# Transposes of shifted attention scores split by upper and lower 64 rows, each half into its own PSUM bank

## The reference

```python
x = jnp.roll(input, (-SH, -SH), axis=(1, 2))      # windows of 7 x 7 = 49 tokens, 16 per image
qkv = x @ qkv_weight.T + qkv_bias                 # 8 heads of 8 channels
attn = jnp.einsum('whnd,whmd->whnm', q * scale, k) + relative_position_bias
attn = attn + attn_mask                           # shifted-window mask
attn = jax.nn.softmax(attn, axis=-1)
out = jnp.einsum('whnm,whmd->whnd', attn, v)      # then projection, roll back
```

## Time and profile before

| | |
|---|---|
| Median of 3 runs | 204.85 us (204.46 to 205.53) |
| Profiled execution, its own time | 204.72 us |
| Span of the profiled execution | 202.9 us |
| TensorE busy | 189.9 us, 2827 matmuls |
| Turns (L892) | 256 transposes, 33.1 us busy |
| Exponentials (L583) | 64, 28.4 us busy |
| Values (L912) | 1024 passes, 29.0 us busy |
| Scores (L881) | 512 passes, 28.2 us busy |
| Granted TensorE clock | 0.999 |

### The profile page before, as it was taken

The page is one execution under the profiler, slowest core; times in us unless marked ns, Lnnn a source line. Parts: engine busy times, 40 slices in busy tenths (PEclk is TensorE's granted clock), DMA queues, the critical chain, the costliest instruction groups (busy, mean ns, idle before and its releaser), DMA issues.

```text
span 202.9 us, 7030 instructions
## 1 busy us (share of the span) xinstructions
PE 189.9 (94%) x2827; PEld 132.7 (65%) x2830; DVE 154.7 (76%) x319; ACT 142.1 (70%) x305; POOL 110.7 (55%) x123
## 2 busy tenths in 40 slices
PE   7769999999999999999999999989979899999994
PEld 2447888888888878788878787645536566443331
DVE  4476689977887877886876977897768848874894
ACT  2148698688778789878887964537746547798880
POOL 0338999958311549823279305925993631635680
PEclk9999999999999999999999999999999999999999
DMA  6980000000000010100010100022132551020124
GB/s 198 438 357 3 3 3 3 3 3 5 0 3 3 3 26 6 40 3 3 3 26 3 43 5 3 3 64 45 26 68 66 122 128 30 20 77 2 44 78 160
DMA packets 6111, 10.77 MB, mean 53 GB/s; under 512 B 960, under 2 KB 5184, under 8 KB 5952
## 3 DMA queue, kind: packets, MB, share of 16 engines
q1 hardware_dynamic: 5648, 9.72, 15.8%
q10 hardware_dynamic: 432, 0.60, 0.9%
HBM read 5.03 MB, written 1.61 MB: 33 GB/s over the span
## 4 chain that ended last, share of the span: by engine, by line
PE 60%; POOL 13%; ACT 11%; issue 6%; DMA 5%; DVE 2%; SPq 2%; POOLq 1%; ACTq 0%; DVEq 0%
PE turned L892 12%; PE scores L881 10%; PE outs L912 10%; PE scores L1021 4%; PE qkv L862 4%; PE qkv L852 4%; PE scores L1037 2%; POOL v L420 2%; DMA xw<-xw_in 2%; POOL h L413 2%; POOL v L418 2%; ACT xs L694 2%; PE outs L936 2%; ACT pt L583 2%; DMA p<-parts 2%
## 5 line engine op out<-in xcount | busy, mean ns | idle before, releaser
L1298 DVE TENSOR_REDUCE mx<-scores 113x16 f32<-113x784 f32 x32 | 30.9, 964 | 6.9 <-PE scores L881 6.6
L374 POOL TENSOR_TENSOR rstd<-ve,mhalf 128x1 f32<-128x1 f32 (+1 forms) x15 | 9.6, 641 | 46.7 <-DVE ve L1264 46.4
L892 PE MATMUL turned<-cst,d 113*113 113x113 f32 x256 | 33.1, 272 | 0.0
L225 POOL TENSOR_TENSOR kex<-ks,cst 128x784 f32<-128x784 f32 (+1 forms) x16 | 23.6, 1475 | 17.3 <-ACT ks L562 17.1
L892 PEld LDWEIGHTS turned<-cst,d 113*113 113x113 f32 x256 | 27.9, 178 | 7.1 <-issue 7.1
L583 ACT ACTIVATE pt<-turned 113x392 f32<-113x392 f32 x64 | 28.4, 496 | 5.7 <-PE turned L892 3.1
L1303 DVE TENSOR_TENSOR d<-scores,mx 113x784 f32<-113x784 f32 x32 | 31.2, 976 | 1.1
L553 ACT ACTIVATE scores<-rel 113x784 f32<-113x784 f32 x32 | 26.2, 818 | 5.7 <-POOL rel L366 3.2
L881 PE MATMUL scores<-kex,qs 32*49 32x196 f32 x512 | 28.2, 332 | 2.0 <-DVE kex L225 1.7
L912 PEld LDWEIGHTS outs<-vsb,pt 113*49 113x49 f32 x1024 | 26.0, 125 | 5.6 <-issue 2.5
L912 PE MATMUL outs<-vsb,pt 113*49 113x18 f32 x1024 | 29.0, 199 | 0.0
(11 more groups left out here) (139 smaller groups left out, 379.0 us busy)
## 6 DMA issues: line engine op xcount, KB each, us to landing
p<-parts SPq DMA_DIRECT2D x14, 112.5 KB, 2.3
x<-x_in SPq DMA_DIRECT2D x1, 1568.0 KB, 10.0
out<-xw SPq DMA_DIRECT2D x8, 196.0 KB, 1.9
xw<-xw_in SPq DMA_DIRECT2D x1, 784.0 KB, 6.7
xs<-xs SPq DMA_DIRECT2D x6, 98.5 KB, 2.1
v2x<-v SPq DMA_DIRECT2D x6, 98.0 KB, 2.1
ker<-ker_in SPq DMA_DIRECT2D x2, 288.0 KB, 10.2
p3x<-parts SPq DMA_DIRECT2D x8, 60.0 KB, 2.0
```

The lines of the kernel that those rows point to most:

```text
L225: return engine.tensor_tensor(kex[:, par, :, a * WT:b * WT], ks[:, a * WT:b * WT].rearrange("p (o t) -> p o t", o=1).broadcast_to([P, 4, n ...
L892: mm = pe.transpose(ps_t[j][0:WK, n * P:n * P + WK], d[0:WK, k % 2, h:h + 2, :].rearrange("p a b -> p (a b)")[:, 0:WK], ident[0:WK, 0:WK])
L1298: dve.tensor_reduce(top, sc, AXX, ALU.max).then_inc(max_done, 1)
```

## The change

A turn becomes one call per pair. It does 16 transposes: for each of 8 couples of blocks one over the partitions 0 to 48 (the one image) into the bank `ps_t[0]`, and one over the partitions 64 to 112 (the other image) into `ps_t[1]`, in alternation. Each result is a block of 49 columns, stored 64 apart. An exponential `expo(k, w)` now reads one bank, which holds one image's queries for all heads and both windows, and writes its 49 columns of every block of `pt`; the layout of `pt` is as before. `t_done` counts one per pair, both exponentials wait for the whole turn, and a turn waits for both exponentials of the pair before.

```diff
--- before.py
+++ after.py
@@ -575,13 +575,13 @@
                         ps_qk[q, 0:NW * C].rearrange("p (a n d) -> p a n d", a=NW, d=HD), ACT.Identity)
                 last.then_inc(v_ready, 1)
 
-            def expo(k, j):
-
-                act.wait_ge(t_done, 2 * k + j + 1)
+            def expo(k, w):
+
+                act.wait_ge(t_done, k + 1)
                 if k >= 2:
                     act.wait_ge(pv_done, k - 1)
-                act.activation(pt[0:WK, k % 2, j].rearrange("p n (w t) -> p n w t", w=2),
-                               ps_t[j][0:WK, :].rearrange("p (n w t) -> p n w t", n=4, w=2)[:, :, :, 0:WT],
+                act.activation(pt[0:WK, k % 2, :, :, w * WT:(w + 1) * WT].rearrange("p j n t -> p (j n) t"),
+                               ps_t[w][0:WK, :].rearrange("p (n t) -> p n t", n=NH)[:, :, 0:WT],
                                ACT.Exp).then_inc(exp_done, 1)
 
             def evac_att(R):
@@ -883,15 +883,16 @@
                                            start=False, stop=True, skip_group_check=True)
                 mm.then_inc(s_done, 1)
 
-            def turn(k, j):
+            def turn(k):
                 pe.wait_ge(sub_done, k + 1)
                 if k > 0:
-                    pe.wait_ge(exp_done, 2 * k - 1 + j)
-                for n in range(4):
-                    h = 8 * j + 2 * n
-                    mm = pe.transpose(ps_t[j][0:WK, n * P:n * P + WK],
-                                      d[0:WK, k % 2, h:h + 2, :].rearrange("p a b -> p (a b)")[:, 0:WK],
-                                      ident[0:WK, 0:WK])
+                    pe.wait_ge(exp_done, 2 * k)
+                for n in range(NH):
+                    for w in range(2):
+                        q = slice(64 * w, 64 * w + WT)
+                        mm = pe.transpose(ps_t[w][0:WK, 64 * n:64 * n + WT],
+                                          d[q, k % 2, 2 * n:2 * n + 2, :].rearrange("p a b -> p (a b)")[:, 0:WK],
+                                          ident[q, q])
                 mm.then_inc(t_done, 1)
 
             def values(k):
@@ -953,8 +954,7 @@
                 R, p = k // 2, k % 2
                 g, r = R // NW, R % NW
 
-                turn(k, 0)
-                turn(k, 1)
+                turn(k)
                 if p == 0 and R + 2 < NR:
                     proj_qk(R + 2)
                 if p == 0 and R >= 2:
@@ -1137,16 +1137,14 @@
             pe.wait_ge(w2_ready, 2)
             pe.wait_ge(ld_late, 16)
             pe.wait_ge(g12_ready, 1)
-            turn(NP - 2, 0)
-            turn(NP - 2, 1)
+            turn(NP - 2)
             project(NR - 3)
             values(NP - 3)
             conv1_quad(0)
             sums_quad(0)
             pe.wait_ge(gn_copied, nth(1, 2))
             gather(NR - 2)
-            turn(NP - 1, 0)
-            turn(NP - 1, 1)
+            turn(NP - 1)
             values(NP - 2)
             values(NP - 1)
             sums_quad(1)
@@ -1299,7 +1297,7 @@
                 dve.wait_ge(max_done, k + 1)
 
                 if k >= 2:
-                    dve.wait_ge(t_done, 2 * k - 2)
+                    dve.wait_ge(t_done, k - 1)
                 dve.tensor_tensor(d[0:WK, s].rearrange("p (j m) t -> p j m t", j=2)[:, :, :, 0:WT], sc,
                                   top.rearrange("p j (m o) -> p j m o", o=1).broadcast_to([WK, 2, NH, WT]),
                                   ALU.subtract).then_inc(sub_done, 1)
```

## The result

The kernel after takes 207.25 us (median of 4 runs, 207.06 to 208.21), beside 204.82 (204.46 to 205.53) for the kernel before: a ratio of 1.0126, 95% interval 1.0103 to 1.0150. 208.7 was predicted, with a range of 203.8 to 213. The profiled execution takes 207.32 with a span of 205.4, so 2.5 us more span than before. In the kernel after, the turn's line is L893; the attention's TensorE lines behind it are one higher (L926 for L925), those of the later blocks are the same, and VectorE's are two lower.

A forecast was written before the change was run, and what follows sets the result against it. TensorE, busy 94% of the span, was taken as the bound. Terms 1.9 + 1.6 + 0.45 - 0.05 - 0.1 + 0.1 = 3.9 us on 204.72 gave 208.6, as a median 208.7; range 203.8 to 213, forecast's own 207.3 to 210.3.

The forecast's parts named there:

- The cadence: Turn's transposes on TensorE: 8 steps of a side-by-side pair at 0.099 us, so a turn stays 0.79 us.
- The pause and the open load: TensorE after a turn: shape change pauses, next line's load no longer hidden; loss 0.13 to 0.14 us before L852.
- even turn: Turns followed by L852 or L936 on the chain, pairs 2 to 28: 14 x 0.135 = 1.9 us lost.
- odd turn: Turns followed by L925's transposes, pairs 3 to 29: 0.09 to 0.135 each, taken 0.115; 14 x 0.115 = 1.6 us lost.
- Mix turns: Turns behind a small full-array matmul (L816 or L983), 5 before 121 us: a new pause, 5 x 0.09 = 0.45 us.
- The waits: Both exponentials wait for all 16 transposes, the first 0.34 us later; V's wait for Q's copy just covered, by 0.05.
- the two late stretches: 68 to 75 and 97 to 104 us, ScalarE late: one turn's 0.135 hides in each, exponential adds 0.1; together -0.1.
- The end: End of the loop: ScalarE's absolute values, at 123.72 before, wait for pair 30's later exponentials: +0.1 us.
- the pause is paid: Denied by rival 2: 64-row transposes leave the array's shape, no pause, no change; 203.4 to 204.8 us, chance 0.06.
- the halves go side by side: Denied by rival 3: halves don't overlap or alternate with a pause, 1.58 us per turn; 231 us, chance 0.07.
- the issue of the instructions: Rival 4: TensorE can't issue 16 loads and 16 matmuls in 0.79 us; 214.5 us, chance 0.04.
- The first rival: Faster: the shorter stream sets the turn's pace, 0.46 us a turn, pair's step at most 0.082; about 199.5 us, chance 0.11.

## Why the prediction was right

The measured median lies well inside the stated range of 203.8 to 213, and 0.05 below the forecast's own range of 207.3 to 210.3.

*The cadence.* Right to the digit: loads in pairs, pairs 0.099 us apart, set by 113 loaded columns on each half; a turn keeps its 0.79. The argument behind it was the form of L1120's loads, and it carried over to transposes. One reading was off: the 0.099 of before was taken for a stream with the load hidden beside it, and with faster loads that stream runs at 0.097, so load and stream were nearly alike, the load a little longer.

*The pause and the open load.* Right, and slightly large. Next load at 0.92 forecast, 0.93 measured; 0.135 forecast for an even turn, 0.12 to 0.13 measured; 0.115 for an odd turn, taken in the middle of 0.09 to 0.135, 0.097 measured: behind the pause, L926's first load lies open for only 0.06 (its second starts 0.06 after it), about what the turn's last stream is shorter by. These are the mis-sized terms: 1.36 for 1.6 in the odd turns, and 1.59 for 1.8 in the even ones. Half of what the even turns fall short by is turn 8: in the kernel before, L852 waits there for the scale of the convolution (`aw`, from VectorE, done at 44.40 us) and starts 0.90 after the turn's first load instead of 0.79, and the pause hides in that. Mix turns: 0.09 forecast and measured, but for the one behind L983. That the pause comes from the change of the array's shape is read from timelines: it is there behind the turn in every kernel with halves and in none with the whole array, but no run changed the shape alone.

*The waits.* Right for the kernel after, with too general a reason. The first exponential was forecast 1.02 after the turn's start and comes at 1.04; V does not wait for Q's copy in ordinary turns. That the same waits by themselves cost 1.46 us in the old form, at the mixes and in ScalarE's late stretches, the prediction did not see. In the new form TensorE is itself late at the mixes, and in the two late stretches the wait takes the pause's place: 0.10 and 0.09 on the way to turns 17 and 25 in place of 0.13, about as forecast in sum (-0.1 together; -0.07 measured). A third such place, on the way to turn 5 (0.10), was not named.

*The end.* Absolutes at 127.6 forecast, 127.06 measured, mostly because the turns lost less. The forecast's largest error lies behind it, outside all its terms: 0.87 us of DMA wait that was in the kernel before and went away. The wait did not swallow a delay: TensorE and the DMAs' first issue came 3.4 us later alike (155.79 to 159.17), but the group then landed within 4.03 us and not 5.09. Without it the span would have grown by 3.4, beside 3.9 forecast. The row with the wait stood in the trace of before and was not weighed.

*The rivals.* In the kernel after, none came true: the pairs' step is above 0.082 us, the pause is paid, and the halves go side by side at the pace of the loads; the issue of the instructions sets no such limit, since the kernel with 66 columns issues as many in 0.47 us. The first rival had the right condition: below 0.082 us a pair the change gains, and at 0.057 it does. That this gives 199.55 us, where the rival's working gave 199.5, is in part luck, as the missing wait at L1021 is in it. Against this rival the prediction held that loads follow columns, and that was read too widely: L925's load of 128 columns takes 142 ns, L892's of 113 takes 178, and this was the sign of the even count. The Trainium skill (TensorEngine Tiling, Theoretical Speedup) has up to 2x for a dimension of at most 64. Measured from the turn's first load to the next line's, the halves give 0.79/0.93 = 0.85x with 113 columns, 0.79/0.58 = 1.36x with 114, and 0.79/0.47 = 1.7x with 66, which leave out data.

## What to carry to other kernels

Splitting these transposes over half the rows took their stream from 113 to 49 columns and left their load at 113: before such a split, find out which of the two sets the cadence, and what the next line loses when the array's shape changes. When a load of one shape is slower than one with more columns, try the neighbouring counts before anything else. A delay worked out up to some point reaches the end unchanged only if the waits behind it stay as they are, so read these rows, too, and what else was being transferred at that time.

## What the runs showed of the hardware

The load of an fp32 transpose, in the five counts that were run, depends on whether its column count is even: 175 ns in the profile for 113 and 177 for 115, but 109 for 66, 133 for 114 and 139 for 128. By the cadence of pairs, a loaded column costs 0.099/113 = 0.88 ns and 0.100/115 = 0.87 where the count is odd, 0.057/114 = 0.50 and 0.062/128 = 0.48 where it is even. An even count does not make L852's fp32 loads, which are no transposes, as short: 128 columns, 189 ns. Nor does it speed the stream, which stays near 0.86 ns a column with 113 or 114.

Two halves of the array load side by side: 16 loads of 49 rows by 113 columns take 0.87 us, as 8 of 113 rows did. Behind such a turn the next line's load starts 0.93 us after the turn's first, where it was 0.79 without the change of the array's shape.
